# Mixture-of-experts block: the gated product computed twice instead of computed and rounded, and one weight subtraction moved into the gate

## The chip, the cores and the metric

One core of a Trainium2 chip runs the whole program. The metric is the device time in microseconds (us), the median over several executions. TensorE multiplies matrices, VectorE and ScalarE and GpSimd work elementwise, and SyncE issues transfers between HBM and the on-chip memory (SBUF). TensorE's products land in PSUM.

## What is computed

Two layers of cross attention and feed-forward over 4096 tokens of width 256. The part that is changed is the last one, a mixture of 8 experts with the two best experts per token:

```
logits = x @ gate_w + gate_b                      # x: 4096 x 256
top_w, top_idx = top_k(softmax(logits), 2); top_w = top_w / sum(top_w)
h   = silu(x @ w1[e]) * (x @ w3[e])               # w1, w3: 256 x 1024
out = sum over the two experts e of  weight_e * (h @ w2[e])   # w2: 1024 x 256
x   = x + tanh(g_ffn[1]) * out
```

## The kernel before

Three stages follow one another: the first layer, the second cross attention, and the experts. The change touches only the experts.

The tokens are sorted by expert into 39 blocks (`NBLK`) of 256 rows (`BLK`); each block has one expert, whose three weight matrices (1 MB each, 128 x 2048 numbers) are loaded afresh for it. The multiplications keep fp32 precision by splitting each operand in a high part, rounded to fp32r, and a low part, the rest, and running three passes of matmuls: high times low, low times high, high times high (`three_passes`, L1680 to L1684). So every operand needs two elementwise steps: a rounded copy, and a subtraction of the copy from the original.

For block j, in buffers that alternate (p = j mod 2):

- SyncE loads the rows of the block (`e_x`) and the raw weights (`m_raw0` to `m_raw2` for w1, w3, w2). A raw buffer is loaded again once its low part has been made (`lo_done[n]`).
- ScalarE makes the high parts of the three weights of block j + 1 (`high_part`, L1345) during block j: behind the silu of f = 1, 3 and 5.
- The low parts of the weights of block j + 1 (`low_part`, L1349): that of w1 by VectorE in the gate of block j, behind the first pair; that of w3 by VectorE in `x_low` (L1772), which runs after the gate of block j and belongs to block j + 1 already; that of w2 by GpSimd, between its fetch and its store of block j.
- TensorE runs `hidden(j)` (8 chunks f of 12 matmuls, 96 in all, into four PSUM banks; from the fifth chunk on each waits until VectorE has read the chunk four before, `gated_done`), then `turn(j + 1)` (4 transposes of the next rows), then `project(j)` (4 pairs of 12 matmuls, each of which waits for one pair of chunks of the gated product, `g_parts`), and goes on with `hidden(j + 1)`, which waits for `lo_done[0]`, `lo_done[1]` and `x_lo_done`.
- ScalarE computes silu of chunk f into one of two buffers (L1742), each once VectorE has used the chunk two before (`gated_done`).
- VectorE's queue for a block is: `gate(j)`, `x_low(j + 1)`, `add_y(j)`. `gate` handles the chunks in pairs: two products silu times PSUM (L1781), one rounding of both (L1784, the high part), one subtraction (L1786, the low part). The sequence is written out by hand: an instruction waits only for the semaphores ahead of it, but everything behind it waits with it.
- GpSimd's queue is: `fetch(j)` gathers the rows of the output that block j adds to, by indirect transfers (L1640), and may do so only when the stores of block j - 1 have landed (`y_out`); `low_part` of w2 for block j + 1; `store(j)` (L1647), which waits for `add_y(j)` (`y_left`).

Of the kernel before, what the change touches and what calls it, by code (L numbers as in the profile page):

```python
# [8 lines left out]
ALU, ACT, AX = mybir.AluOpType, mybir.ActivationFunctionType, mybir.AxisListType  # L9
# [9 lines left out]
FC = FF // P  # L19
NE, TOPK = 8, 2  # L20
BLK = 256
# [1280 lines left out]
def experts(nc, M1, X, tg, ident_f, stats, mu_rs, xs, out):  # L1302
# [10 lines left out]
    with ExitStack() as ctx:  # L1313
# [33 lines left out]
        def low_part(eng, j, p, n):  # L1347
            eng.wait_ge(hi_done[n], j + 1)
            eng.tensor_tensor(w_lo[p][n][:, :, :], raw[n][:, :, :], w_hi[p][n][:, :, :].bitcast(F32), ALU.subtract)\  # L1349
                .then_inc(lo_done[n], 1)  # L1350
# [3 lines left out]
        with ExitStack() as route:  # L1354
# [43 lines left out]
            @block.sync  # L1398
            def _(sp):
                sp.dma_start(gw[:, :, :], gate_w.rearrange("(c p) n -> p c n", p=P)).then_inc(w_in, 16)  # L1400
                sp.dma_start(gb[:, :], bcast_rows(gate_b, NE)).then_inc(w_in, 16)
                sp.dma_start(rows.rearrange("(t p) d -> p t d", p=P), X[:, :, :]).then_inc(x_out, 16)
                sp.wait_ge(pos_done, 1)
                load_weights(sp, 0)
                load_weights(sp, 1)
                for n in range(3):
                    sp.wait_ge(w_raw_in[n], 32)
                sp.wait_ge(x_out, 16)
# [174 lines left out]
        with ExitStack() as run:  # L1583
# [9 lines left out]
            silu = two("silu", [P, BLK])  # L1593
            gated = sb("gated", [P, 2, BLK])
            g_hi, g_lo = sb("g_hi", [P, FC, BLK], F32R), sb("g_lo", [P, FC, BLK], F32R)
            yb = two("y", [P, BT, D])
            ps_x = [ps[:, p, :] for p in range(2)]
            ps_h = [ps[:, 2 + n, :] for n in range(4)]
# [159 lines left out]
            @block.vector  # L1758
            def _(dve):
                steps = Steps(dve, chain)  # L1760

                def x_low(j, p):

                    dve.wait_ge(x_hi_done, j + 1)
                    dve.tensor_tensor(x_lo[p][:, :, :].rearrange("p c n -> p (c n)"), ps_x[p],  # L1765
                                      x_hi[p][:, :, :].bitcast(F32).rearrange("p c n -> p (c n)"), ALU.subtract)\
                        .then_inc(x_lo_done, 1)
                    if not (isinstance(j, int) and j < 2):
                        dve.wait_ge(y_out, 16 * BT * (j - 1))
                    dve.tensor_copy(label[p][:, :, :].bitcast(I32), xb[p][:, :, D:WIDE].bitcast(I32)).then_inc(labelled, 1)  # L1770
                    if not (isinstance(j, int) and j == 0):
                        low_part(dve, j, p, 1)  # L1772

                def gate(j, i, p, following=True):

                    steps.start(FC // 2 * j)
                    for f in range(0, FC, 2):
                        for k in range(2):
                            n = FC * j + f + k
                            dve.wait_ge(silu_done, n + 1)  # L1780
                            dve.tensor_tensor(gated[:, k, :], silu[k][:, :], ps_h[(f + k) % 4][:, BLK:2 * BLK], ALU.mult)\  # L1781
                                .then_inc(gated_done, 1)
                        dve.wait_ge(gated_done, n + 1)
                        steps.done(dve.tensor_copy(g_hi[:, f:f + 2, :], gated[:, :, :]))  # L1784
                        steps.wait()
                        dve.tensor_tensor(g_lo[:, f:f + 2, :], gated[:, :, :], g_hi[:, f:f + 2, :].bitcast(F32), ALU.subtract)\  # L1786
                            .then_inc(g_parts, 1)
                        if f == 0 and following:
                            low_part(dve, j + 1, 1 - p, 0)
                        dve.wait_ge(g_parts, FC // 2 * j + f // 2 + 1)  # L1790

                def add_y(j, p):
                    dve.wait_ge(before_in, 16 * BT * (j + 1))
                    for n in range(BT):
                        dve.wait_ge(y_ps, BT * j + n + 1)
                        dve.scalar_tensor_tensor(out=yb[p][:, n, :], in0=ps_y[n], scalar=label[p][:, n, 0:1], in1=yb[p][:, n, :],  # L1796
                                                 op0=ALU.mult, op1=ALU.add).then_inc(y_left, 1)

                x_low(0, 0)
                gate(0, 0, 0)  # L1800
                x_low(1, 1)
                add_y(0, 0)
                gate(1, 0, 1)
                x_low(2, 0)
                add_y(1, 1)
                with dve.Fori(1, LAST // 2) as i:
                    gate(2 * i, i, 0)
                    x_low(2 * i + 1, 1)
                    add_y(2 * i, 0)
                    gate(2 * i + 1, i, 1)  # L1810
                    x_low(2 * i + 2, 0)
                    add_y(2 * i + 1, 1)
                gate(LAST, LAST // 2, 0, False)
                add_y(LAST, 0)
# [53 lines left out]
```

## Time and profile before

| What | Value |
|---|---|
| median of 3 runs | 2627.19 us (2626.43 to 2630.02) |
| the profiled execution | 2611.73 us, span 2610.0 us |
| TensorE busy | 2107.1 us (81%), mean granted clock 0.911 |
| VectorE busy | 1935.4 us (74%) |
| ScalarE, GpSimd busy | 1022.2 us, 1016.1 us (39% each) |
| first matmul of `hidden(0)` to first of `hidden(38)` | 1777.67 to 2583.78 us |

Engines are named PE (TensorE's matmuls), PEld (its weight loads), DVE (VectorE), ACT (ScalarE), POOL (GpSimd) and SP (SyncE). Busy shares are averages over the stages; what a change in the experts is worth shows only in the repeating pattern of one block there. Names like `e_g_hi` are the tile `g_hi` of the block loop; `m_hi` and `e_hi` are the same weight part in the two alternating buffers. A row of a timeline is the start, the duration, the engine, the line and the operation; in brackets stands how long the engine sat idle before it and who released it.

### The profile page before, as it was taken

To read this page: it belongs to the slowest core of one execution; us is meant where nothing else is said; L and a number is where in the kernel's file an instruction comes from. 1 tells how busy PE (TensorE), PEld (TensorE's weight loads), DVE (VectorE), ACT (ScalarE), POOL (GpSimd) and SP (SyncE) were. 2 spreads that over 40 slices of the span, in tenths; PEclk is the share of its full clock that TensorE was granted. 3 is DMA by queue.
4 is the path that set the end of the run, shared out by engine and by line. 5 is a ranking of instruction groups with operands and counts; after the bars stand their busy time and mean duration, and the time that the engine had idled before them with its cause. 6 is when DMAs were issued, how large, how long until landed. Compare 5 with 4: busy or idle time off the path is not lost. (4 is left out here: it accounts for less than half of the span.)

```text
span 2610.0 us, 40439 instructions
## 1 busy us (share of the span) xinstructions
PE 2107.1 (81%) x13358; PEld 1479.3 (57%) x13358; DVE 1935.4 (74%) x3725; ACT 1022.2 (39%) x1581; POOL 1016.1 (39%) x554
## 2 busy tenths in 40 slices
PE   5898899747788888898888898406888888888887
PEld 3566666633234343434343435306888888888887
DVE  7999999837686867686768743605888888888886
ACT  2343344322355453545444453203444444444443
POOL 7988888622112030302021101273444444443343
PEclk9899999876799999999999998558999999999999
DMA  7000000021001010101010001233555555555552
GB/s 283 10 9 9 11 9 9 1 61 30 23 19 33 9 41 2 41 3 39 12 31 21 1 1 65 90 129 130 190 181 175 191 181 182 178 180 181 180 176 83
DMA packets 124788, 208.89 MB, mean 80 GB/s; under 512 B 9981, under 2 KB 88430, under 8 KB 124660
## 3 DMA queue, kind: packets, MB, share of 16 engines
q1 hardware_dynamic: 114024, 181.97, 20.9%
q0 software_dynamic: 10624, 25.26, 2.7%
q8 instruction: 73, 1.20, 0.2%
q14 instruction: 55, 0.45, 0.1%
q10 hardware_dynamic: 12, 0.01, 0.0%
HBM read 177.58 MB, written 33.18 MB: 81 GB/s over the span
## 5 line engine op out<-in xcount | busy, mean ns | idle before, releaser
L1218 DVE CUSTOM_DVE_ANT_0 x_dump<-x_ps,x_bias_q 128x512 bf16<-128x512 f32 x512 | 343.0, 690 | 66.5 <-PE x_ps L906 47.9
L1072 ACT ACTIVATE x_PT<-x_ps 128x1024 f32<-128x1024 f32 x256 | 255.0, 1021 | 311.0 <-PE x_ps L916 311.0
L843 POOL TENSOR_TENSOR x_rs<-x_ve,x_half 128x3 f32<-128x3 f32 x32 | 28.0, 876 | 719.6 <-DVE x_ve L1151 719.6
L1742 ACT ACTIVATE e_silu<-m_ps 128x256 f32<-128x256 f32 x312 | 118.8, 381 | 479.2 <-PE m_ps L1683 479.2
L906 PE MATMUL x_ps<-x_KS,x_QS 96*128 96x512 bf16 x512 | 207.5, 413 | 36.5 <-DVE x_mx L1218 33.4
L1781 DVE TENSOR_TENSOR e_gated<-e_silu,m_ps 128x256 f32<-128x256 f32 x312 | 122.4, 419 | 124.3 <-ACT e_silu L1742 115.3
L915 PE MATMUL x_ps<-x_bias_k,x_ident_b 128*128 128x512 bf16 x512 | 198.7, 388 | 19.2 <-issue 10.2
L1784 DVE CAST e_g_hi<-e_gated 128x512 fp32r<-128x512 f32 x156 | 209.4, 1343 | 5.3
L1683 PE MATMUL m_ps<-e_x_lo,m_hi 128*128 128x256 f32 x640 | 182.8, 286 | 26.0 <-issue 24.3
L1683 PE MATMUL m_ps<-e_x_lo,e_hi 128*128 128x256 f32 x608 | 180.3, 296 | 25.7 <-issue 25.7
L916 PE MATMUL x_ps<-x_QS,x_KS 99*128 99x512 bf16 x512 | 198.4, 388 | 0.0
L1683 PE MATMUL m_ps<-e_x_hi,m_hi 128*128 128x256 f32 x640 | 181.1, 283 | 0.0
L1683 PE MATMUL m_ps<-e_x_hi,m_lo 128*128 128x256 f32 x640 | 181.1, 283 | 0.0
L1640 POOL DMA_INDIRECT e_y<-out_dram,e_label x78 | 87.6, 1123 | 235.0 <-DMA out_dram<-e_y,e_label 207.9
L1683 PE MATMUL m_ps<-e_x_hi,e_lo 128*128 128x256 f32 x608 | 178.2, 293 | 0.0
L1683 PE MATMUL m_ps<-e_x_hi,e_hi 128*128 128x256 f32 x608 | 177.7, 292 | 0.0
L906 PEld LDWEIGHTS x_ps<-x_KS,x_QS 96*128 96x128 bf16 x512 | 49.4, 99 | 220.6 <-DVE x_mx L1218 182.0
L1647 POOL DMA_INDIRECT out_dram<-e_y,e_label x78 | 78.8, 1010 | 237.7 <-DVE e_y L1796 225.8
L259 POOL TENSOR_TENSOR a_pool_pv<-a_e,a_v 128x2304 f32<-128x2304 f32 x32 | 162.5, 5078 | 0.0
L1683 PEld LDWEIGHTS m_ps<-e_x_lo,e_hi 128*128 128x128 f32 x608 | 121.9, 201 | 29.6 <-issue 29.6
L1683 PEld LDWEIGHTS m_ps<-e_x_lo,m_hi 128*128 128x128 f32 x640 | 121.4, 190 | 29.8 <-issue 29.8
L931 PE MATMUL x_ps<-x_PT,x_V 128*17 128x512 f32 x1024 | 135.8, 602 | 0.3 <-ACT x_PT L1072 0.3
(275 smaller groups left out, 6043.2 us busy)
## 6 DMA issues: line engine op xcount, KB each, us to landing
m_raw<-in_L_ffn_w_dram SPq DMA_DIRECT2D x117, 1024.0 KB, 5.2
expert_in<-a_blank SPq DMA_DIRECT2D x1, 10062.0 KB, 28.4
e_x<-expert_in SPq DMA_DIRECT2D x39, 258.0 KB, 8.1
x_mask_q<-in_mask_dram SPq DMA_DIRECT2D x32, 256.0 KB, 2.7
x_mask_k<-in_maskT_dram SPq DMA_DIRECT2D x32, 256.0 KB, 2.9
a_cT<-in_ctxT_dram SPq DMA_DIRECT2D x32, 128.0 KB, 2.2
x_cT<-in_ctxT_dram SPq DMA_DIRECT2D x32, 128.0 KB, 2.1
out_dram<-X SPq DMA_DIRECT2D x1, 4096.0 KB, 13.6
```

The source lines that it names most:

```text
L259: pool.tensor_tensor(heads(pool_pv[:, :], PV_POOL), probabilities(e_[t % 2][:, PV_OWN * H:], PV_POOL), values(v_sb[t % 3][:, :], PV_POOL), ...
L906: pe.matmul(bank, QS[bp][0:HROWS, h, q * P:(q + 1) * P], KS[bp][0:HROWS, h, :], start=True, stop=True).then_inc(ready, 1)
L915: pe.matmul(ps_st[pr][:, k, :], ident_b[:, :], bias_k[bp][:, kc, :], start=True, stop=False)
L916: mm = pe.matmul(ps_st[pr][:, k, :], KS[bp][:, h, kc * P:(kc + 1) * P], QS[bp][:, h, :], start=False, stop=True)
L931: mm = pe.matmul(ps_o[32 * j:32 * j + VW, :], V[bp][:, kc, 4 * g + j, :], PT[u % 2][:, j, :], start=(kc == 0), stop=(kc == TPB - 1))
L1072: act.activation(PT[u % 2][:, 2 * pr:2 * pr + 2, :], ps_st[pr], ACT.Exp).then_inc(exp_done[pr], 1)
L1218: dve.tensor_tensor_reduce(out=dump[i % 2][:, :], in0=bank, in1=bias_q[:, q, :], scale=1.0, scalar=NEG, op0=ALU.add, op1=ALU.max, accum_ou ...
L1640: pool.indirect_dma_start(out=yb[p][:, n, :], out_offset=None, in_=rows, in_offset=tokens(p, n), bounds_check=T - 1, oob_is_err=False).the ...
L1683: mm = pe.matmul(out, left[a], right[b], start=first and n == 0, stop=last and n == 2)
L1742: act.activation(silu[f % 2][:, :], ps_h[f % 4][:, 0:BLK], ACT.Silu).then_inc(silu_done, 1)
L1781: dve.tensor_tensor(gated[:, k, :], silu[k][:, :], ps_h[(f + k) % 4][:, BLK:2 * BLK], ALU.mult)\
L1784: steps.done(dve.tensor_copy(g_hi[:, f:f + 2, :], gated[:, :, :]))
```

## The change

In `gate`, each product is computed twice from the same two sources: once in fp32 into `gated`, once with fp32r output straight into `g_hi`. The rounding of the pair (`tensor_copy`, L1784) goes. `gated_done`, which lets TensorE and ScalarE reuse the PSUM bank and the silu buffer, is now counted by the second of the two products. The low part of w3 for block j + 1 is no longer made in `x_low(j + 1)` but in `gate(j)`, behind the third pair (f = 4); that of w1 stays behind the first pair (f = 0).

```diff
 def x_low(j, p):
     ...
     dve.tensor_copy(label[p][:, :, :].bitcast(I32), xb[p][:, :, D:WIDE].bitcast(I32)).then_inc(labelled, 1)
-    if not (isinstance(j, int) and j == 0):
-        low_part(dve, j, p, 1)
 
 def gate(j, i, p, following=True):
-    steps.start(FC // 2 * j)
+    steps.start(FC * j)
     for f in range(0, FC, 2):
         for k in range(2):
             n = FC * j + f + k
             dve.wait_ge(silu_done, n + 1)
-            dve.tensor_tensor(gated[:, k, :], silu[k][:, :], ps_h[(f + k) % 4][:, BLK:2 * BLK], ALU.mult)\
+            steps.done(dve.tensor_tensor(gated[:, k, :], silu[k][:, :], ps_h[(f + k) % 4][:, BLK:2 * BLK], ALU.mult))
+            dve.tensor_tensor(g_hi[:, f + k, :], silu[k][:, :], ps_h[(f + k) % 4][:, BLK:2 * BLK], ALU.mult)\
                 .then_inc(gated_done, 1)
+        steps.wait()
         dve.wait_ge(gated_done, n + 1)
-        steps.done(dve.tensor_copy(g_hi[:, f:f + 2, :], gated[:, :, :]))
-        steps.wait()
         dve.tensor_tensor(g_lo[:, f:f + 2, :], gated[:, :, :], g_hi[:, f:f + 2, :].bitcast(F32), ALU.subtract)\
             .then_inc(g_parts, 1)
-        if f == 0 and following:
-            low_part(dve, j + 1, 1 - p, 0)
+        if f in (0, 4) and following:
+            low_part(dve, j + 1, 1 - p, f // 4)
         dve.wait_ge(g_parts, FC // 2 * j + f // 2 + 1)
```

## Rows read from the trace of the kernel before

**Rows 1.** The stretch of 38 blocks: busy time and count by engine, TensorE's clock

```profile
1777.67:2583.78 806.11, 704.53 (x5625) 689.74 (x5625) 667.61 (x835) 333.10 (x457) 337.15 (x188) 0.97 0.52 177
```

**Rows 2.** Groups from 1620 us to 2605 us: count, busy us, mean ns, idle before

```profile
L1784 DVE CAST e_g_hi<-e_gated 128x512 fp32r<-128x512 f32 x156 | 209.4, 1343 | 5.3
```

**Rows 3.** VectorE's timeline of two blocks, around 1854 us and 1863 us

```profile
1854.47 5.49 DVE L1786 TENSOR_TENSOR e_g_lo<-e_gated,e_g_hi 128x512 fp32r<-128x512 f32 x1
1860.00 0.69 DVE L1765 TENSOR_TENSOR e_x_lo<-m_ps,e_x_hi 128x512 fp32r<-128x512 f32 x1
...
1866.60 0.42 DVE L1781 TENSOR_TENSOR e_gated<-e_silu,m_ps 128x256 f32<-128x256 f32 x1 [0.93 <-ACT e_silu L1742]
...
1868.40 2.29 DVE L1349 TENSOR_TENSOR e_lo<-m_raw,e_hi 128x2048 fp32r<-128x2048 f32 x1 [0.20 <-ACT e_hi L1345]
1870.61 0.75 DVE L1781 TENSOR_TENSOR e_gated<-e_silu,m_ps 128x256 f32<-128x256 f32 x2
...
1871.85 0.69 DVE L1786 TENSOR_TENSOR e_g_lo<-e_gated,e_g_hi 128x512 fp32r<-128x512 f32 x1
1872.67 0.75 DVE L1781 TENSOR_TENSOR e_gated<-e_silu,m_ps 128x256 f32<-128x256 f32 x2
...
1875.59 4.25 DVE L1784 CAST e_g_hi<-e_gated 128x512 fp32r<-128x512 f32 x1
1879.87 0.69 DVE L1786 TENSOR_TENSOR e_g_lo<-e_gated,e_g_hi 128x512 fp32r<-128x512 f32 x1
...
1881.28 2.29 DVE L1349 TENSOR_TENSOR e_lo<-m_raw,e_hi 128x2048 fp32r<-128x2048 f32 x1
1883.48 0.87 DVE L1796 SCALAR_TENSOR_TENSOR e_y<-m_ps,e_label,e_y 128x256 f32<-128x256 f32 x2
```

**Rows 4.** GpSimd's timeline of the same two blocks

```profile
1854.84 4.56 POOL L1349 TENSOR_TENSOR m_lo<-m_raw,m_hi 128x2048 fp32r<-128x2048 f32 x1
...
1874.94 4.61 POOL L1349 TENSOR_TENSOR e_lo<-m_raw,e_hi 128x2048 fp32r<-128x2048 f32 x1
```

**Rows 5.** TensorE's timeline of the same two blocks, the matmuls that follow a gap

```profile
1860.02 0.58 PE L1683 MATMUL m_ps<-e_lo,e_g_hi 128*128 128x256 f32 x1 [2.60 <-DVE e_g_lo L1786]
...
1863.06 0.36 PE L1683 MATMUL m_ps<-e_x_lo,m_hi 128*128 128x256 f32 x1
...
1880.62 0.39 PE L1683 MATMUL m_ps<-m_lo,e_g_hi 128*128 128x256 f32 x1 [1.24 <-DVE e_g_lo L1786]
...
1883.66 0.36 PE L1683 MATMUL m_ps<-e_x_lo,e_hi 128*128 128x256 f32 x1 [1.35 <-issue]
```

**Rows 6.** ScalarE's timeline, the third high part of the block at 1863 us

```profile
1872.15 1.91 ACT L1345 ACTIVATE e_hi<-m_raw 128x2048 fp32r<-128x2048 f32 x1
```

**Rows 7.** The first layer: a VectorE subtraction of two SBUF tiles, and GpSimd beside it

```profile
37.99 4.39 DVE L596 TENSOR_TENSOR a_w_lo<-a_w,a_w_hi 128x2048 fp32r<-128x2048 f32 x1
...
37.45 2.79 POOL L245 TENSOR_TENSOR a_pool_qk<-a_q,a_k 128x1536 f32<-128x1536 f32 x1
40.20 4.41 POOL L247 TENSOR_TENSOR a_pool_qk<-a_q,a_k 128x1280 f32<-128x1280 f32 x1
54.80 2.38 POOL L247 TENSOR_TENSOR a_pool_qk<-a_q,a_k 128x1280 f32<-128x1280 f32 x1
```

**Rows 8.** The line of the product, all 312: minimum, median, maximum ns

```profile
L1781 DVE TENSOR_TENSOR e_gated<-e_silu,m_ps x312: 410/420/424, 1781.0 to 2595.9; 128x256 f32<-128x256 f32 x156
```

**Rows 9.** Chain that ended last: two runs of 96 matmuls, and the last block

```profile
1863.06 11.64 PE m_ps L1683 x96
...
2096.69 14.00 PE m_ps L1683 x96
...
2583.78 17.34 PE m_ps L1683 x144
```

**Rows 10.** Stretches of 1 us: busy PE, PEld, DVE, ACT, POOL; granted clock; DMA

```profile
1861.00:1862.00 1.00, 1.00 (x7) 1.00 (x6) 1.00 (x1) 0.00 (x0) 0.00 (x0) 0.50 0.00 0
...
2101.00:2102.00 1.00, 1.00 (x7) 1.00 (x7) 0.00 (x0) 0.00 (x0) 0.00 (x0) 0.52 0.96 272
```

## The prediction

> **What bounds the kernel now.** I read the stage table first: the change lies in the experts only, so everything before 1777.67 us stays. From there to the first matmul of the last block 38 blocks take 806.11 us, 21.21 us each, in which TensorE is busy 704.53 us and VectorE 667.61 us, both over 80% [rows 1]. Neither is full, so the next view is the list of groups: the rounding of a pair has a mean of 1343 ns over 156 [rows 2], though its usual duration is 0.43 us. The timeline shows why. Three of the four roundings of a block take about 0.43 us; the fourth takes 4.25 us, from 1875.59 to 1879.84 [rows 3], and ends 0.3 us after GpSimd's subtraction for w2, which ran from 1874.94 to 1879.55 [rows 4]. The rounding did not work for 4 us; it was held by GpSimd's operation.
>
> The reader should see what hangs on that. TensorE has by then done three of the four pairs of `project` and waits for the last low part: 1.24 us idle up to 1880.62, then 12 matmuls, then 1.35 us more until 1883.66 [rows 5]. The second wait is called "issue", but it ends just after VectorE's w3 subtraction, 1881.28 to 1883.57 [rows 3]: `hidden` waits for `lo_done[1]`. So one block is a ring: `add_y` ends, GpSimd stores, the store lands, the fetch is issued, GpSimd's w2 subtraction runs, VectorE is held until it ends, then the rest of VectorE's queue up to `add_y`. From the end of one `add_y` (1863.7) to GpSimd's subtraction (1874.94) are 11.2 us.
>
> **The timetable of a block before.** Times from the first matmul of `hidden`, 1863.06 [rows 5], which I call 0: second product of pair 0 at 3.54 [rows 3]; w1 subtraction 5.34 to 7.63, pair 1 of products at 7.55, its low part 8.79 to 9.48, pair 2 of products from 9.61 [rows 3]; ScalarE's high part of w2 done at 11.00 [rows 6]; GpSimd's subtraction 11.88 to 16.49 [rows 4]; held rounding to 16.78, last low part to 17.50, w3 subtraction to 20.51, `add_y` to 21.29 [rows 3]; next `hidden` at 20.60 [rows 5].
>
> **Part 1: the products twice, no rounding.** A product takes 0.42 us alone and two in a row 0.75 us, so each further one costs 0.33 us [rows 3]. Four products are 3 x 0.33 + 0.42 = 1.41 us, where two products and the rounding were 0.75 + 0.03 + 0.43 = 1.21 us. That the output is fp32r is not shown for a product; the subtraction that writes fp32r has the price of its width, 0.69 us for 512 columns, so I add nothing. VectorE thus pays 0.20 us more per pair where it is not held, and `gated_done` comes 0.3 us later, which delays neither the PSUM banks (chunk 6 needs product 2, which is done at 8.3; it starts at 6 x 1.42 = 8.5) nor ScalarE by more than 0.3 us.
>
> What of the stall? A product reads one SBUF tile and one PSUM bank, and none of the 312 took more than 424 ns [rows 8], though the last pair, right ahead of the held rounding at 1875.59, ran beside GpSimd's subtraction, which began at 1874.94 [rows 3, 4]. So the four products of pair 3 will not be held. But the low part comes behind them and reads two SBUF tiles. In the block before that one the fourth rounding got through ahead of GpSimd, and there the low part itself took 5.49 us instead of 0.69, until 0.56 us after GpSimd's end at 1859.40 [rows 3, 4]. The first layer has the same: a w1 subtraction of the same shape as here took 4.39 us, not 2.29, beside one GpSimd product, and the next GpSimd product took 4.41 us, not 2.38 [rows 7, 3]. So two-tile operations of the two engines take turns, whole instruction by whole instruction. Removing the rounding moves the hold by one instruction and gains 0.3 us.
>
> The Trainium skill, SBUF — State Buffer, "Who interferes with whom", says the same as a rule: a VectorE instruction with two SBUF inputs contends with a GpSimd instruction that reads SBUF, the second to issue blocks fully, and one with at most one SBUF input outside the two-port modes does not. It speaks against this change, and by it the part-2 sum below would come out as from the rows; the trace agrees with it (5.49 us against 0.69).
>
> **Part 2: the w3 subtraction goes into the gate.** On its old place it cost TensorE the 1.35 us [rows 5]. On its new one it too reads two SBUF tiles, and stands in front of pair 3. The new timetable: second product of pair 0 at 3.54, three instructions from there to 4.29, low part to 5.0; w1 subtraction waits for ScalarE as before, 5.34 to 7.63; pair 1 products 7.55 to 8.96, low part to 9.68; pair 2 products 9.81 (0.13 behind a low part, as at 1872.67 [rows 3]) to 11.22, low part 11.25 to 11.94; the w3 subtraction is then ready at 11.9 to 12.0. GpSimd's is ready at 11.9: the fetch as before, and ScalarE's high part at 11.0 + 0.3. That is a tie by the rows, and I say GpSimd goes first, for two reasons. At 1854.47 VectorE's low part started 0.37 us ahead of GpSimd's recorded start and still waited [rows 3, 4]. And any slow start of `hidden` (below) puts VectorE back, not the fetch.
>
> With GpSimd first: its subtraction runs from 11.94 to 16.5 (4.56 us [rows 4]); the w3 subtraction ends at 16.5 + 2.29 - 0.13 = 18.66 (the held low part ended 0.56 behind GpSimd, 0.13 less than its 0.69); products of pair 3 18.59 to 20.0; low part 20.03 to 20.72. Before, this point was 17.50. TensorE goes on at 20.77.
>
> TensorE's last 12 matmuls take 12 x 0.12 = 1.5 us at full clock and 12 x 0.21 = 2.6 us at half; with 0.15 us of starts `hidden` follows 1.7 or 2.75 us later, now without a wait for w3 or x. `add_y` follows about 0.5 us behind, 0.1 to 0.2 us sooner than before, which leaves the fetch where it was. Loads of the raw weights start earlier than now for w3 and at the same point for w2: they are hidden, as before.
>
> **TensorE's clock.** Behind 2.60 us of idleness the 12 matmuls ran at granted clock 0.50, the 1.2 GHz level (1861 to 1862 us) [rows 5, 10], and the next `hidden` took its full-speed 11.64 us; where TensorE had idled twice, `hidden` began at half clock, was so until about 2101.9, and took 14.00 us [rows 9, 10], 5.2 us of work at half speed. Now TensorE idles from 16.2 (matmuls 36 of `project`) to 20.77, 4.6 us, in every block. So I take the half clock for the 12 matmuls as given: 20.72 + 0.05 + 2.75 + 0.1 = 23.6 us a block. What reaches into `hidden` is unknown: between nothing (as at 1863.06) and 2.6 us (5.2 less the 12 matmuls'), which delays silu and VectorE by up to 1.2 us, of which about 0.8 reaches the end: then GpSimd starts ahead of the low part of pair 2, which is held in its place. 23.6 to 24.4; I take the middle, 24.0 us.
>
> **The sum.** 38 x (24.0 - 21.21) = +106 us. The last block has no weight parts to make and is bound by TensorE, 17.34 us for 144 matmuls [rows 9]; unchanged. On the profiled execution 2611.7 + 106 = 2718 us. The median of the runs is 15.5 us above that execution, an offset that I keep: 2733 us.
>
> **The rivals.**
>
> - *The same order, but the clock holds, or VectorE wins the tie.* If the 12 matmuls run at full clock, a block is 20.72 + 1.7 = 22.4 us. If the w3 subtraction goes first (12.0 to 14.3), GpSimd runs 14.3 to 18.9, pair 3's products run beside it, the last low part ends at 18.9 + 0.56 = 19.5, and with half clock a block is 19.5 + 2.9 = 22.4 us too. Either gives 38 x 1.2 = +45 us, 2672 us. For the second speaks the tie; against it that it idles TensorE 3.3 us, so the next `hidden` starts slow and GpSimd wins there.
> - *Both of these together*: 19.5 + 1.7 = 21.2 us, no change.
> - *The hold goes: faster.* If GpSimd's subtraction did not hold a two-tile subtraction that is already queued, the w3 subtraction would end at 14.3, pair 3 at 15.7, its low part at 16.4, just when TensorE is through its 36 matmuls (16.2), and TensorE never waits: 18.1 us a block, 38 x -3.1 = -118 us, 2509 us. It decides at one point: whether the two-tile instruction behind GpSimd's start runs 2.29 us or waits. It would need GpSimd's subtraction to start after 16.4 or to be shared. For it: VectorE's busy time alone would fit into 18 us. Against it: 5.49 us and 4.39 us [rows 3, 7].
> - *More of the clock.* If TensorE's half clock covers more than 5.2 us of work each time, up to 24.9 us a block, +140 us, 2767 us.
>
> **How the numbers follow.** Chances: the forecast 0.62 (23.3 to 24.6 us a block, 2707 to 2756 us); one of the two at 22.4 us 0.20; both together 0.04; the hold goes or shrinks enough to gain 0.09; more of the clock 0.05. A measurement of this kernel tells 0.2% (5 us) from no change, the spread of its three runs being 0.14%. The range from 2665 to 2770 us holds the forecast, the 22.4 us cases and most of the last. Faster 0.09, within 0.2% 0.04, slower 0.87.
>
> **What would show it.** After the change: no rounding group; 624 products at 0.42 us, none held; the w3 subtractions of VectorE with a mean of 5 to 7 us, or low parts of up to 5 us, ending 0.5 us (low parts) or 2.2 us (subtractions) behind GpSimd's end; a wait of TensorE for the last low part of 4 to 5 us in each block, and no "issue" wait ahead of `hidden`; granted clock in the stage well under the 0.97 of [rows 1]; a block of 24 us. The prediction is wrong if the w3 subtraction takes 2.29 us in most blocks: then either VectorE won the tie, and the last low part is long, or there is no hold, and nothing is.

## The result: 3.4% slower, as forecast

The changed kernel takes 2713.18 us (median of 4, 2710.74 to 2717.86) where the kernel before took 2626.81 us in the same comparison: ratio 1.0336, 95% interval 1.0308 to 1.0364. The forecast was 2733 us, slower, range 2665 to 2770; between the medians it was +106 us, and +86 us was measured. Its profiled execution took 2715.13 us with a span of 2713.4 us, 103 us more than the profiled one of before. The first matmul of `hidden(0)` comes at 1782.46 us, 4.8 us later than before (nothing there was changed), and the 38 blocks to `hidden(38)` take 903.91 us, 23.79 us each against 21.21, together 97.8 us more:

```profile
1782.46:2686.37 903.91, 743.36 (x5625) 728.26 (x5625) 718.70 (x987) 337.36 (x457) 375.98 (x188) 0.93 0.47 158
```

This is the stretch of [rows 1] after the change: busy time by engine, then TensorE's clock, down from 0.97 to 0.93. The groups of the experts that answer to [rows 2 and 8] (count, busy us, mean ns, idle before), and the waits between 1782 and 2690 us (total, times, longest):

```profile
L1784 DVE TENSOR_TENSOR e_g_lo<-e_gated,e_g_hi 128x512 fp32r<-128x512 f32 x156 | 264.7, 1697 | 16.2
L1779 DVE TENSOR_TENSOR e_gated<-e_silu,m_ps 128x256 f32<-128x256 f32 x312 | 129.6, 415 | 119.5 <-ACT e_silu L1742 100.4 <-issue 14.5
L1780 DVE TENSOR_TENSOR e_g_hi<-e_silu,m_ps 128x256 fp32r<-128x256 f32 x312 | 128.7, 413 | 0.0
```

```profile
PE m_ps L1683 <- DVE e_g_lo L1784: 160.6, 74, 4.5
...
POOL e_y L1640 <- DMA out_dram<-e_y,e_label: 84.0, 36, 2.6
...
POOL e_lo L1349 <- ACT e_hi L1345: 46.3, 19, 10.2
```

The rounding is gone; its 4 us are now in the low part, whose mean rose to 1697 ns. The products have their plain price. TensorE waits for low parts 160.6 us, twice per block. And GpSimd, which in 30 of the 38 blocks came to its subtraction straight from a fetch before, now waits for ScalarE in all 38.

One block shows the order; it begins at 1880.27. The pairs are counted from 0, so pair 2 is the third (f = 4). VectorE, GpSimd, ScalarE's high part of w2 and TensorE's resumptions, as in [rows 3 to 6]:

```profile
1886.66 2.29 DVE L1349 TENSOR_TENSOR e_lo<-m_raw,e_hi 128x2048 fp32r<-128x2048 f32 x1 [0.25 <-ACT e_hi L1345]
...
1891.20 0.42 DVE L1779 TENSOR_TENSOR e_gated<-e_silu,m_ps 128x256 f32<-128x256 f32 x1
...
1892.72 5.05 DVE L1784 TENSOR_TENSOR e_g_lo<-e_gated,e_g_hi 128x512 fp32r<-128x512 f32 x1
1897.69 2.28 DVE L1349 TENSOR_TENSOR e_lo<-m_raw,e_hi 128x2048 fp32r<-128x2048 f32 x1
1899.89 0.41 DVE L1779 TENSOR_TENSOR e_gated<-e_silu,m_ps 128x256 f32<-128x256 f32 x1
...
1901.40 0.69 DVE L1784 TENSOR_TENSOR e_g_lo<-e_gated,e_g_hi 128x512 fp32r<-128x512 f32 x1
```

```profile
1886.60 1.04 POOL L1640 DMA_INDIRECT e_y<-out_dram,e_label  x1 [2.35 <-DMA out_dram<-e_y,e_label]
1887.94 1.90 POOL L1640 DMA_INDIRECT e_y<-out_dram,e_label  x1 [0.30 <-issue]
1892.65 4.57 POOL L1349 TENSOR_TENSOR e_lo<-m_raw,e_hi 128x2048 fp32r<-128x2048 f32 x1 [2.81 <-ACT e_hi L1345]
```

```profile
1890.65 1.91 ACT L1345 ACTIVATE e_hi<-m_raw 128x2048 fp32r<-128x2048 f32 x1
```

```profile
1897.82 0.39 PE L1683 MATMUL m_ps<-m_lo,e_g_hi 128*128 128x256 f32 x1 [1.60 <-DVE e_g_lo L1784]
1902.14 0.39 PE L1683 MATMUL m_ps<-m_lo,e_g_hi 128*128 128x256 f32 x1 [2.63 <-DVE e_g_lo L1784]
```

GpSimd started at 1892.65, 0.07 us ahead of the low part of pair 2, which ended 0.55 us behind GpSimd. The w3 subtraction, four products and one more low part follow in a row, from 1897.69 to 1902.09, 4.4 us in which nothing is held any more and TensorE has only the third pair to work on. In 36 of the 38 blocks the low part of pair 2 was held like this (5.03 to 5.06 us long) and the w3 subtraction behind it took its plain 2.28 us; in the first two the w3 subtraction was held (6.7 us). Stretches of 1 us of TensorE's clock, as in [rows 10]:

```profile
1903.00:1904.00 1.00, 1.00 (x8) 1.00 (x8) 0.49 (x1) 0.00 (x0) 0.00 (x0) 0.64 1.06 434
...
1905.00:1906.00 1.00, 1.00 (x7) 1.00 (x6) 0.00 (x0) 0.00 (x0) 0.38 (x1) 0.50 1.08 379
1906.00:1907.00 1.00, 1.00 (x8) 1.00 (x8) 0.00 (x0) 0.15 (x1) 0.69 (x2) 0.66 1.10 354
1907.00:1908.00 1.00, 1.00 (x11) 1.00 (x10) 0.74 (x2) 0.23 (x1) 0.95 (x1) 1.00 1.11 351
```

After the second gap the clock falls to the 1.2 GHz level while TensorE works again, for some 3 us, part in the last matmuls of `project`, part in `hidden`.

### The profile page after: what moved, and what is told of

It is laid out like the page before. It is cut to its first block and busy times, and to the rows that moved or that the text cites. A ratio compares the mean times of both kernels' runs of the same rounds, so it can differ in the third digit from the quotient of the medians.

```text
span 2713.4 us, 40674 instructions
## 1 busy us (share of the span) xinstructions
PE 2140.8 (79%) x13281; PEld 1520.2 (56%) x13358; DVE 1988.5 (73%) x3881; ACT 1027.8 (38%) x1581; POOL 1056.1 (39%) x554
## 3 DMA queue, kind: packets, MB, share of 16 engines
q1 hardware_dynamic: 114024, 181.97, 20.5%
## 5 line engine op out<-in xcount | busy, mean ns | idle before, releaser
L1784 DVE TENSOR_TENSOR e_g_lo<-e_gated,e_g_hi 128x512 fp32r<-128x512 f32 x156 | 264.7, 1697 | 16.2
L1779 DVE TENSOR_TENSOR e_gated<-e_silu,m_ps 128x256 f32<-128x256 f32 x312 | 129.6, 415 | 119.5 <-ACT e_silu L1742 100.4
L916 PE MATMUL x_ps<-x_QS,x_KS 99*128 99x512 bf16 x512 | 198.1, 387 | 19.3 <-ACT x_KS L1048 10.3
L1683 PE MATMUL m_ps<-e_x_lo,m_hi 128*128 128x256 f32 x640 | 189.6, 296 | 1.5 <-DVE e_x_lo L1765 1.5
L1683 PE MATMUL m_ps<-e_x_hi,m_lo 128*128 128x256 f32 x640 | 188.7, 295 | 0.0
L1683 PE MATMUL m_ps<-e_x_hi,m_hi 128*128 128x256 f32 x640 | 187.8, 293 | 0.0
L915 PE MATMUL x_ps<-x_bias_k,x_ident_b 128*128 128x512 bf16 x435 | 168.7, 388 | 7.5 <-issue 7.4
L1640 POOL DMA_INDIRECT e_y<-out_dram,e_label x78 | 128.4, 1647 | 107.7 <-DMA out_dram<-e_y,e_label 84.0
L1683 PE MATMUL m_ps<-m_lo,e_g_hi 128*128 128x256 f32 x320 | 100.7, 315 | 80.1 <-DVE e_g_lo L1784 80.1
L1683 PE MATMUL m_ps<-e_lo,e_g_hi 128*128 128x256 f32 x304 | 96.3, 317 | 80.4 <-DVE e_g_lo L1784 80.4
```

The costliest lines, as they stand in the source:

```text
L915: pe.matmul(ps_st[pr][:, k, :], ident_b[:, :], bias_k[bp][:, kc, :], start=True, stop=False)
L916: mm = pe.matmul(ps_st[pr][:, k, :], KS[bp][:, h, kc * P:(kc + 1) * P], QS[bp][:, h, :], start=False, stop=True)
L1640: pool.indirect_dma_start(out=yb[p][:, n, :], out_offset=None, in_=rows, in_offset=tokens(p, n), bounds_check=T - 1, oob_is_err=False).the ...
L1683: mm = pe.matmul(out, left[a], right[b], start=first and n == 0, stop=last and n == 2)
L1779: steps.done(dve.tensor_tensor(gated[:, k, :], silu[k][:, :], ps_h[(f + k) % 4][:, BLK:2 * BLK], ALU.mult))
```

## The experiments

Block lengths are the mean over the 38 blocks. "Last low part" is when VectorE ends it, from the block's first `hidden` matmul, also a mean.

| Kernel | Median us (before beside it) | Ratio (95%) | Block us | Last low part |
|---|---|---|---|---|
| before | 2626.81 | | 21.21 | 18.0 |
| the change | 2713.18 (2626.81) | 1.0336 (1.0308 to 1.0364) | 23.79 | 21.6 |
| products_only | 2634.75 (2624.36) | 1.0040 (1.0025 to 1.0054) | 21.81 | 18.7 |
| move_only | 2716.99 (2624.36) | 1.0350 (1.0333 to 1.0367) | 23.93 | 21.2 |
| after_memset | 2493.72 (2624.36) | 0.9497 (0.9481 to 0.9513) | 17.96 | 16.4 |
| after_quarters | 2665.85 (2624.36) | 1.0157 (1.0140 to 1.0175) | 22.55 | 20.2 |
| after_f6 | 2654.39 (2615.78) | 1.0145 (1.0128 to 1.0162) | 22.29 | 19.3 |
| after_f2 | 2612.83 (2615.78) | 0.9995 (0.9981 to 1.0008) | 21.17 | 19.3 |
| products_quarters | 2645.61 (2615.78) | 1.0105 (1.0084 to 1.0127) | 22.08 | 18.9 |
| before_quarters | 2615.99 (2615.78) | 1.0000 (0.9990 to 1.0010) | 21.08 | 17.8 |
| before_waits | 2534.34 (2613.84) | 0.9711 (0.9679 to 0.9743) | 19.12 | 15.5 |
| products_waits | 2514.04 (2613.84) | 0.9628 (0.9597 to 0.9660) | 18.62 | 15.1 |
| f2_waits | 2553.70 (2613.84) | 0.9774 (0.9753 to 0.9794) | 19.61 | 18.0 |
| after_waits | 2676.34 (2619.41) | 1.0228 (1.0206 to 1.0250) | 22.83 | 20.3 |

**Which half of the change costs? products_only.** From the changed kernel:

```diff
 def x_low(j, p):
     ...
+    if not (isinstance(j, int) and j == 0):
+        low_part(dve, j, p, 1)
 def gate(j, i, p, following=True):
         ...
-        if f in (0, 4) and following:
-            low_part(dve, j + 1, 1 - p, f // 4)
+        if f == 0 and following:
+            low_part(dve, j + 1, 1 - p, 0)
```

> Each product twice and no rounding, but the w3 subtraction back in x_low: part 1 of the change alone. Theory A (the hold by GpSimd's subtraction and the place of the w3 subtraction set the time): the hold moves from the fourth rounding to the fourth low part and ends 0.3 us sooner, so about 20.9 us a block against 21.2 before, 2605 to 2625 us. Rival B (VectorE's added work sets the time: 8 more products of 0.33 us for 4 roundings of 0.43 us, +0.9 us a block, so that the move is harmless): 2650 to 2665 us.

Measured 0.40% slower: neither. Two blocks of VectorE's low parts, and GpSimd beside them:

```profile
1964.54 5.82 DVE L1786 TENSOR_TENSOR e_g_lo<-e_gated,e_g_hi 128x512 fp32r<-128x512 f32 x1
...
1987.18 0.69 DVE L1786 TENSOR_TENSOR e_g_lo<-e_gated,e_g_hi 128x512 fp32r<-128x512 f32 x1
...
1989.51 3.66 DVE L1786 TENSOR_TENSOR e_g_lo<-e_gated,e_g_hi 128x512 fp32r<-128x512 f32 x1
```

```profile
1964.21 1.01 POOL L1640 DMA_INDIRECT e_y<-out_dram,e_label  x1 [0.31 <-issue]
1965.24 4.55 POOL L1349 TENSOR_TENSOR e_lo<-m_raw,e_hi 128x2048 fp32r<-128x2048 f32 x1
...
1988.02 4.59 POOL L1349 TENSOR_TENSOR m_lo<-m_raw,m_hi 128x2048 fp32r<-128x2048 f32 x1
```

In the second block the low part of the fourth pair is held, as theory A had it, and the block takes 20.5 us. In the first the low part of the third pair (f = 4) is caught though it began 0.70 us ahead of GpSimd's recorded start; the fourth pair's products then come behind the hold and the block takes 22.65 us. The two cases have 19 blocks each, with means of 20.9 and 22.7 us. Because four products are 0.2 us longer than two and a rounding, the low part of that pair comes late enough to be caught. So the products cost little by themselves, but they moved a tie.

**move_only.** From the kernel before: the w3 subtraction taken out of `x_low` and put into `gate` with `f in (0, 4)`, as in the diff of the change; rounding and single product stay.

> The rounding kept, one product each, and the w3 subtraction in the gate behind the third pair: part 2 alone. Theory A: GpSimd's subtraction still goes ahead of the w3 subtraction, which is queued ahead of the fourth pair: about 23.6 us a block, 2700 to 2725 us. Rival B: the move takes TensorE's 1.35 us wait away and costs nothing: 19.9 us a block, about 2580 us.

3.5% slower, as theory A had it, and no less than the whole change: the move is the cost, as long as GpSimd's subtraction holds. Here GpSimd catches the w3 subtraction itself, in all 38 blocks:

```profile
1982.76 4.91 POOL L1349 TENSOR_TENSOR e_lo<-m_raw,e_hi 128x2048 fp32r<-128x2048 f32 x1 [2.57 <-ACT e_hi L1345]
```

```profile
1983.14 6.69 DVE L1349 TENSOR_TENSOR e_lo<-m_raw,e_hi 128x2048 fp32r<-128x2048 f32 x1
```

**Is it GpSimd that holds? after_memset.** In `low_part`, for GpSimd's w2, the subtraction is left out (the low part of w2 is zero) and three fills of about the same total length stand in its place; the lines that declare `alone` and `spare` are not shown:

```diff
         def low_part(eng, j, p, n):
             eng.wait_ge(hi_done[n], j + 1)
+            if n == 2 and eng is nc.gpsimd:
+                stand_alone(eng, alone)
+                for c in range(2):
+                    eng.memset(spare[c][:, :], 0.0)
+                mm = eng.memset(w_lo[p][n][:, :, :].bitcast(F32), 0.0)
+                mm.then_inc(lo_done[n], 1)
+                return
```

> The changed kernel with GpSimd's w2 subtraction left out and three fills of 128x2048 in its place (about 5 us of GpSimd that read no SBUF; the low part of w2 is zero, so the third pass of project adds nothing). Theory A: nothing holds VectorE; low parts 0.69 us and w3 subtractions 2.29 us throughout, TensorE waits for neither, 18.1 to 18.6 us a block, 2500 to 2530 us. Rival C (VectorE's order and its total work make the block long, whatever GpSimd does): low parts and w3 subtractions short too, but TensorE still waits over 2 us for the last low part, above 2600 us.

```profile
1957.91 3.55 POOL L1354 MEMSET m_spare<- 128x2048 f32 x2 [1.52 <-ACT m_hi L1347]
1961.41 1.81 POOL L1355 MEMSET m_lo<- 128x2048 f32 x1
```

```profile
1957.91 0.69 DVE L1793 TENSOR_TENSOR e_g_lo<-e_gated,e_g_hi 128x512 fp32r<-128x512 f32 x1
1958.52 2.28 DVE L1358 TENSOR_TENSOR m_lo<-m_raw,m_hi 128x2048 fp32r<-128x2048 f32 x1
```

GpSimd is as busy (5.3 us), but its fills read nothing, and VectorE's subtractions run beside them at their plain durations: of the 114 that overlapped a fill none was held. A block is 17.96 us, near the 18.1 us of the prediction's rival. So it is GpSimd's subtraction that holds, and the changed order fits under TensorE if nothing is held. Which property of the subtraction does it is not shown. That it reads SBUF is not enough: in the second cross attention of the kernel before, a GpSimd operation with one SBUF input had the whole of a VectorE subtraction of two SBUF tiles beside it, ten times, and it took its plain 0.69 us each time:

```profile
603.74 1.97 POOL L855 TENSOR_SCALAR x_bias_k<-x_mask_k 128x512 bf16<-128x512 int32 x1
```

```profile
604.76 0.69 DVE L1179 TENSOR_TENSOR x_rest<-x_qk,x_hi 128x512 f32<-128x512 f32 x1
```

**Shorter holds: after_quarters.** The changed kernel with GpSimd's w2 subtraction cut in four (`FC` is 8):

```diff
         def low_part(eng, j, p, n):
             eng.wait_ge(hi_done[n], j + 1)
+            if n == 2 and eng is nc.gpsimd:
+                for c in range(0, FC, FC // 4):
+                    at = slice(c, c + FC // 4)
+                    mm = eng.tensor_tensor(w_lo[p][n][:, at, :], raw[n][:, at, :], w_hi[p][n][:, at, :].bitcast(F32), ALU.subtract)
+                mm.then_inc(lo_done[n], 1)
+                return
```

> The changed kernel with GpSimd's w2 subtraction cut in four instructions of 128x512, about 1.15 us each. Theory A (the engines take turns instruction by instruction): VectorE gets in between two quarters, no instruction of it is held for more than 1.3 us, the last low part ends near 17.5 to 18.5 us instead of 21, and a block takes 19.5 to 20.5 us: 2560 to 2600 us. Rival D (VectorE waits until GpSimd has nothing left queued): holds of 4 to 5 us stay, 2690 us or more.

```profile
1990.26 7.48 POOL L1352 TENSOR_TENSOR m_lo<-m_raw,m_hi 128x512 fp32r<-128x512 f32 x4 [1.46 <-ACT m_hi L1345]
```

```profile
1990.33 1.76 DVE L1790 TENSOR_TENSOR e_g_lo<-e_gated,e_g_hi 128x512 fp32r<-128x512 f32 x1
1992.01 3.38 DVE L1355 TENSOR_TENSOR m_lo<-m_raw,m_hi 128x2048 fp32r<-128x2048 f32 x1
...
1996.82 1.47 DVE L1790 TENSOR_TENSOR e_g_lo<-e_gated,e_g_hi 128x512 fp32r<-128x512 f32 x1
```

The holds are 0.8 to 1.1 us, as expected, but the kernel is 1.6% slower than before, not faster, and the last low part comes at 20.2 us, not at 17.5 to 18.5: between one pair and the next the w3 subtraction now takes 3.4 us, TensorE waits 3.0 us in one piece, and 24 of 38 blocks have a slow start of `hidden` (over 12 us). Shorter holds take away half of the loss. The other half is three of them in a row with the w3 subtraction in the middle, ahead of the last pair. The place by itself is no loss: after_memset has the same order, nothing held, and a block of 17.96 us.

**The place of the w3 subtraction: after_f6 and after_f2.** One line of the changed kernel:

```diff
-                        if f in (0, 4) and following:
-                            low_part(dve, j + 1, 1 - p, f // 4)
+                        if f in (0, 6) and following:
+                            low_part(dve, j + 1, 1 - p, f // 6)
```

and the same with `(0, 2)` and `f // 2`.

> The changed kernel with the w3 subtraction behind the fourth pair (f = 6) instead of the third. Theory A (what costs is that the w3 subtraction stands between GpSimd's subtraction and the last pair): the last low part comes within 1 us of GpSimd's end again and the block goes back to that of the products alone, 21.2 to 21.9 us: 2620 to 2650 us. Rival E (two subtractions of VectorE inside one gate are too much wherever they stand): 23.5 us a block or more, 2700 us.

> The changed kernel with the w3 subtraction behind the second pair (f = 2). It is then through before GpSimd's can begin (ScalarE's w2 high part is ready at about 11.3 us), but pair 2's low part is held in its place. Theory A: GpSimd 12.0 to 16.6 us, low part of pair 2 to 17.1, products and low part of pair 3 to 19.3, a block of 21.0 (full clock) to 22.2 us (half clock in the last matmuls): 2619 to 2665 us. Rival E: as the changed kernel, 2700 us.

Behind the fourth pair the kernel is 1.45% slower, a little above theory A's band and far from rival E; the low part of the third pair is caught in 34 of 38 blocks there. Behind the second pair the change is no loss at all (0.9995; 2613 us, where theory A had 2619 at the least):

```profile
2025.74 5.05 POOL L1349 TENSOR_TENSOR m_lo<-m_raw,m_hi 128x2048 fp32r<-128x2048 f32 x1 [1.46 <-ACT m_hi L1345]
```

```profile
2024.08 2.29 DVE L1349 TENSOR_TENSOR m_lo<-m_raw,m_hi 128x2048 fp32r<-128x2048 f32 x1
...
2027.79 3.54 DVE L1784 TENSOR_TENSOR e_g_lo<-e_gated,e_g_hi 128x512 fp32r<-128x512 f32 x1
```

Now it is GpSimd that waits: its 5.05 us are 0.5 longer than its own time, since the w3 subtraction was under way, and only the third low part is held.

**Quarters where GpSimd comes from its fetch: products_quarters and before_quarters.** The edit of after_quarters, in products_only and in the kernel before.

> Products twice, no rounding, the w3 subtraction in x_low as in the kernel before, GpSimd's w2 subtraction in four quarters. Theory A: low parts are held for at most 1.3 us, the last is ready near 15 us, before TensorE has done its 36 matmuls (16.2), and only w3's subtraction, some 3.4 us long between quarters, is waited for: 18.5 to 19.5 us a block, 2520 to 2560 us. Rival D (shorter holds, but as many of them as quarters, so that the sum stays): 2600 us or more.

> The kernel before with only GpSimd's w2 subtraction in four quarters: the roundings are kept. Theory A: the fourth rounding and its low part are held for up to 1.3 us each, the last low part ready near 16 us; 18.5 to 19.7 us a block, 2520 to 2570 us, within 0.5% of the version with the products twice. Rival F (the rounding, which uses more of the shared path than a subtraction, is held until GpSimd is through): no gain, 2610 us or more.

Theory A failed in both, and the times came out as the rivals D and F had them. In products_quarters:

```profile
2056.11 1.01 POOL L1646 DMA_INDIRECT e_y<-out_dram,e_label  x1 [0.31 <-issue]
2057.14 4.96 POOL L1352 TENSOR_TENSOR e_lo<-m_raw,e_hi 128x512 fp32r<-128x512 f32 x4
```

```profile
2056.53 6.13 DVE L1792 TENSOR_TENSOR e_g_lo<-e_gated,e_g_hi 128x512 fp32r<-128x512 f32 x1
```

Four quarters in 4.96 us, back to back, and VectorE held through all four. In after_quarters they took 7.48 us with VectorE in between. The difference in the rows is what came before: there GpSimd had waited for ScalarE, here it went on from the fetch. before_quarters has blocks of both kinds: in the nine where GpSimd waited for ScalarE, its quarters took 8.07 to 8.23 us and the last low part 1.66. Nor is it the rounding alone that is held, as rival F had it: products_quarters has none, and its low part was held.

**Making GpSimd wait: before_waits, products_waits, f2_waits, after_waits.** Each quarter now waits for a semaphore that the one ahead raises, in four kernels. Against the quarters above, with c counted from 0 to 3:

```diff
+                    if c:
+                        eng.wait_ge(part_done, (4 - 1) * (j - 1) + c)
                     mm = eng.tensor_tensor(w_lo[p][n][:, at, :], ...)
+                    if c < 4 - 1:
+                        mm.then_inc(part_done, 1)
```

> The kernel before with GpSimd's w2 subtraction in four quarters, each of which waits for a semaphore that the one ahead of it raises. Theory A2 (a GpSimd instruction lets VectorE in only where GpSimd itself waits; instructions that stand ready behind a fetch run through as one): now the fourth rounding and its low part are held for at most 1.3 us each, a block takes 19.3 to 20.0 us, 2% to 3% less than before: 2550 to 2580 us. Rival G (what let VectorE in between was GpSimd's late start, not its waiting): holds of 4 us or more stay where GpSimd comes from a fetch, no gain.

> Products twice, no rounding, w3 in x_low, quarters with waits. Theory A2: one hold fewer than with the roundings, 18.8 to 19.6 us a block, 2530 to 2560 us. Rival G: as with plain quarters, 22.1 us a block, 2640 us.

> Products twice, no rounding, w3's subtraction behind the second pair, quarters with waits: what the experiments point to as the best. Theory A2: the low parts of pairs 2 and 3 are held for at most 1.3 us each, TensorE waits less than 2 us in all and stays at full clock, 18.5 to 19.3 us a block, 2515 to 2550 us. Rival H (TensorE or ScalarE is the next bound, above that): 20 us a block or more, 2570 us.

> The changed kernel as it is, with GpSimd's w2 subtraction in four quarters with waits: is the whole change worth something once the long hold is gone? Theory A2: the w3 subtraction is held for at most 1.1 us, the last low part comes at 17.3 to 18.3 us, TensorE waits for it 1 to 2 us: 19.3 to 20.3 us a block, 2540 to 2585 us, faster than before but behind the versions that leave w3 in x_low (2534 with the roundings, 2514 without). Rival I (the move pays once nothing is held, as it takes TensorE's wait for w3 away): 18.4 us a block or less, 2505 us.

The first three bear out theory A2: the long holds are gone, also behind a fetch. Two are faster than its figures, though single holds reach 1.5 us in before_waits and 1.9 in products_waits, not 1.3. products_waits, from a fetch:

```profile
2013.98 7.73 POOL L1355 TENSOR_TENSOR e_lo<-m_raw,e_hi 128x512 fp32r<-128x512 f32 x4
```

```profile
2014.71 1.13 DVE L1797 TENSOR_TENSOR e_g_lo<-e_gated,e_g_hi 128x512 fp32r<-128x512 f32 x1
...
2016.93 2.28 DVE L1360 TENSOR_TENSOR e_lo<-m_raw,e_hi 128x2048 fp32r<-128x2048 f32 x1
```

No low part is held for more than 1.9 us anywhere, TensorE keeps its full clock from 1783 to 2480 us (1.00), and the kernel is 3.7% faster than before: the best with the computation whole. Against before_waits, measured beside it, it is 20 us faster: that is what doubling the products is worth once the holds are short. f2_waits, which I had expected to be the best, came out 0.3 us a block above its band and behind both. after_waits missed both expectations: with holds of 1.1 us at most the changed kernel is still 2.3% slower:

```profile
2039.88 1.76 DVE L1795 TENSOR_TENSOR e_g_lo<-e_gated,e_g_hi 128x512 fp32r<-128x512 f32 x1
2041.56 3.37 DVE L1360 TENSOR_TENSOR m_lo<-m_raw,m_hi 128x2048 fp32r<-128x2048 f32 x1
...
2046.36 1.59 DVE L1795 TENSOR_TENSOR e_g_lo<-e_gated,e_g_hi 128x512 fp32r<-128x512 f32 x1
```

It is after_quarters again: GpSimd had waited for ScalarE in both, so the waits add nothing. The order is third low part, w3 subtraction, fourth pair, low part; all three subtractions are lengthened by a quarter or so, which leaves TensorE idle 3.1 us a block, and 27 of 38 blocks begin slow. I had put the last low part at 17.3 to 18.3 us; it is at 19.5 in the blocks that start at full clock and 20.3 on the mean.

## Why the prediction was right

- **The hold moves, it doesn't go** (part 1): right. Low parts of 5.05 us; products never above 424 ns; after_memset shows that GpSimd's subtraction causes it. That this alone gains 0.3 us a block was wrong: products_only loses 0.4%, since the third low part comes 0.5 us later than in [rows 3] and is caught in half the blocks. In the changed kernel this is swallowed by the larger loss. And "whole instruction by whole instruction" holds only in part: behind a fetch four quarters held VectorE as one (products_quarters).
- **Part 2, GpSimd goes first**: it went ahead of the w3 subtraction in all 38 blocks, but not as I had it. I kept the fetch where it was, and so 11.9 us for GpSimd's subtraction. It moved: the first fetch is issued 6.3 us into the block instead of 9.5. GpSimd's subtraction then waits for ScalarE's high part, which waits for VectorE's product of chunk 3, so it comes just ahead of the third low part in 36 blocks. The step "`add_y` follows ..., which leaves the fetch where it was", and with it that the earlier loads are without effect, failed. In each of the seven kernels in which w3's raw buffer was free 3.7 us or more before the next `hidden` (the change, move_only, after_memset, after_quarters, after_f2, f2_waits, after_waits) the first fetch came at 5.9 to 8.0 us (block 0 left out); in the seven where it was freed within 0.8 us of it, at 8.5 to 12.1 us. The store then no longer lands among two 1 MB loads. That fits; no run moved the loads alone.
- **My own sign of being wrong came true**: the w3 subtraction took 2.28 us in 36 of the 38 blocks. I had allowed for two reasons only, VectorE winning the tie or no hold. It was a third: the low part ahead of it was held in its place, which I had foreseen for blocks with a slow start alone. The order on the path, hold, w3 subtraction, four products, low part, stayed what I had summed. TensorE's wait, forecast as 4 to 5 us for the last low part, was split in two, 1.6 and 2.6 us.
- **The timetable was right partly by luck.** At full clock, as I had reckoned it, two errors cancel. In block 29, which starts at 2473.16, GpSimd came at 11.25, not at 11.94, so the third low part was held too:

```profile
2484.41 4.57 POOL L1349 TENSOR_TENSOR m_lo<-m_raw,m_hi 128x2048 fp32r<-128x2048 f32 x1 [1.46 <-ACT m_hi L1345]
```

```profile
2484.48 5.05 DVE L1784 TENSOR_TENSOR e_g_lo<-e_gated,e_g_hi 128x512 fp32r<-128x512 f32 x1
```

From GpSimd's end to the end of the last low part there were 4.9 us against 4.2. So GpSimd was 0.7 us early, the rest 0.65 us longer, and the last low part ended at 20.70, forecast 20.72. In the block at 1880.27, with a slow start, it ended at 21.82 (about 21.5 by my figures), with GpSimd at 12.38.
- **The clock**: I gave the last 12 matmuls the half clock entirely (2.75 us) and `hidden` up to 1.2 us. In the block at 1880.27 they took 1.83 us and `hidden` lost 1.04. Together about 1.2 us, near the 1.05 + 0.4 that I took, but the other way round: the slow stretch lay mostly in `hidden`. The clock did not hold and VectorE did not win the tie, so neither rival at 22.4 us occurred; the faster rival's condition, nothing held, had to be made (after_memset).
- **The sum**: 24.0 us a block forecast, 23.79 measured, 8 us in all. The rest of the miss is the offset: I kept 15.5 us between profiled execution and median, and here the median lies 2 us below the profiled one. Profile against profile it is +103 us, forecast +106, but 4.8 of the 103 lie ahead of the experts, where nothing was changed.

## What to carry to other kernels

When an instruction takes ten times its usual duration, ask who else ran, and whether its successor needs the same thing: here the rounding was removed and the subtraction behind it inherited the wait. Before moving work into a gap, ask what else will hold or be held there and what urgent work is queued behind it. The w3 subtraction cost 3.5% behind the third pair while GpSimd's subtraction held VectorE, and with the doubled products the kernel was level with before when it stood behind the second; with the hold gone, the order that had cost 3.4% was the fastest of all (after_memset, which leaves out the low part of w2). The remedy was on the other engine: GpSimd's long instruction cut in four with a semaphore between each two gave 3.7% with the products doubled and 2.9% without.

## What the hardware showed that I had not expected

- Which of the two engines waits can't be read from the recorded starts alone. Where GpSimd came straight from a fetch in products_only, VectorE's low part was held with a lead of up to 0.72 us (5.85 us long); those with 0.73 us or more, which with their own 0.69 us were through by then, were not. Where GpSimd had waited for ScalarE, VectorE's low part went through with a lead of 0.02 us and GpSimd took 5.13 us.
- Four GpSimd instructions behind a fetch kept VectorE out as one (4.96 to 5.95 us for the four in 63 of 64 blocks); with a semaphore wait between them, or behind a wait for ScalarE, VectorE got in (mostly 7.4 to 8.3 us for the four; 6.2 in f2_waits). What in GpSimd makes the difference stays open.
- VectorE's subtraction also holds GpSimd's fetch. The fetch at 1887.94 took 1.90 us instead of 1.0: the w1 subtraction ran from 1886.66 to 1888.95, and the fetch ended 0.89 us behind it. In after_f2 all 37 fetches that began during a w1 subtraction ended 0.88 to 0.92 us behind its end.
- In the changed kernel `hidden` (to the start of its last matmul) lengthens by some 0.08 us from block to block, from 11.28 us in block 10 to 12.79 in block 28, and jumps back to 11.27 in block 29, as if the fall of the clock wandered through the block. No run here looked into it.
